# The residual buffers of a two-layer graph kernel: b3 and x brought in by two transfers, the second accumulating, instead of one addition on GpSimd

## The reference

```python
def _sage_conv(x, src, dst, W_l, b_l, W_r):
    agg = segment_sum(x[src], dst, num_segments=N_NODES)
    deg = segment_sum(ones, dst, num_segments=N_NODES)
    return (agg / maximum(deg, 1.0)[:, None]) @ W_l + b_l + x @ W_r

h = relu(_sage_conv(x, src, dst, W1_l, b1, W1_r))
h = relu(_sage_conv(h, src, dst, W2_l, b2, W2_r))
out = _layernorm(x + (h @ W3 + b3))
```

## Time and profile before

| | |
|---|---|
| Three runs, median (lowest to highest) | 3070.76 us (3068.34 to 3070.82) |
| The profiled execution: its time, its span | 3069.83 us, 3068.0 us |
| Granted clock of TensorE over the span | 0.974 |
| Busy: PE, DVE, ACT, POOL | 2858.7, 2459.7, 2066.8, 2239.5 us |
| GpSimd's additions for xb (L390) | 196 of 2402 ns, 470.7 us |
| Bytes moved by DMA | 488.23 MB, mean 159 GB/s |

### The profile page before, as it was taken

The page is one execution under the profiler, slowest core; times in us unless marked ns, Lnnn a source line. Parts: engine busy times, 40 slices in busy tenths (PEclk is TensorE's granted clock), DMA queues, the critical chain, the costliest instruction groups (busy, mean ns, idle before and its releaser), DMA issues. The chain is left out here.

```text
span 3068.0 us, 56367 instructions
## 1 busy us (share of the span) xinstructions
PE 2858.7 (93%) x18433; PEld 2560.7 (83%) x18433; DVE 2459.7 (80%) x4095; ACT 2066.8 (67%) x3188; POOL 2239.5 (73%) x1830
## 2 busy tenths in 40 slices
PE   5999999999999999999999999999998887887885
PEld 4898888888888888888888888888888776777775
DVE  5888888888887878878888788787887876777775
ACT  3777677676766777767767676677776655555554
POOL 5777777777777777777777777777776677777776
PEclk9999999999999999999999999999999898989898
DMA  3444444444444445444444444444443655555553
GB/s 128 147 164 152 156 153 155 150 158 157 157 156 147 161 145 164 151 157 151 155 152 159 156 157 155 146 163 145 164 151 128 211 192 174 193 181 188 194 175 118
DMA packets 253118, 488.23 MB, mean 159 GB/s; under 512 B 37615, under 2 KB 165206, under 8 KB 253090
## 3 DMA queue, kind: packets, MB, share of 16 engines
q1 hardware_dynamic: 202498, 387.58, 37.4%
q0 software_dynamic: 50176, 99.91, 10.8%
q10 hardware_dynamic: 416, 0.40, 0.0%
HBM read 284.67 MB, written 206.22 MB: 160 GB/s over the span
## 5 line engine op out<-in xcount | busy, mean ns | idle before, releaser
L494 ACT ACTIVATE h_full<-pair,bias 128x512 f32<-128x512 f32 x784 | 531.5, 684 | 632.0 <-PE pair L866 616.9
L655 DVE TENSOR_TENSOR h_lo<-h_full,h_hi 128x1024 fp32r<-128x1024 f32 x392 | 658.0, 1679 | 174.7 <-ACT h_hi L496 174.7
L390 POOL TENSOR_TENSOR xb<-xn,b_row 128x1024 f32<-128x1024 f32 x196 | 470.7, 2402 | 225.7 <-DVE y L671 223.8
L344 POOL DMA_INDIRECT xe<-in_x_dram,e_stage x392 | 500.7, 1277 | 177.0 <-issue 97.7
L877 PE MATMUL pair<-w_hi,h_hi 128*128 128x256 f32 x1960 | 553.2, 282 | 30.4 <-DVE h_lo L655 28.7
L877 PE MATMUL pair<-w_hi,h_lo 128*128 128x256 f32 x1960 | 543.0, 277 | 0.0
L877 PE MATMUL pair<-w_lo,h_hi 128*128 128x256 f32 x1960 | 542.5, 277 | 0.0
L856 PE MATMUL pair<-ident,xn 128*128 128x128 f32 x2352 | 336.4, 295 | 128.7 <-DMA xn<-h_tab,c_stage 119.4
L856 PEld LDWEIGHTS pair<-ident,xn 128*128 128x128 f32 x2352 | 301.6, 154 | 163.7 <-issue 115.1
L496 ACT CAST h_hi<-h_full 128x1024 fp32r<-128x1024 f32 x392 | 412.7, 1053 | 12.5
L877 PEld LDWEIGHTS pair<-w_hi,h_hi 128*128 128x128 f32 x1960 | 367.8, 188 | 55.4 <-DVE h_lo L655 51.8
(11 more groups left out here) (117 smaller groups left out, 6583.8 us busy)
## 6 DMA issues: line engine op xcount, KB each, us to landing
xn<-in_x_dram SPq DMA_DIRECT2D x196, 512.0 KB, 3.9
out_dram<-o SPq DMA_DIRECT2D x196, 512.0 KB, 2.7
seg<-seg_tab SPq DMA_DIRECT2D x74, 512.0 KB, 5.0
xdb_tab<-xdb SPq DMA_DIRECT2D x49, 512.0 KB, 4.7
h_tab<-src_h SPq DMA_DIRECT2D x49, 512.0 KB
h_tab<-dst_h SPq DMA_DIRECT2D x49, 512.0 KB, 6.2
xn<-h_tab SPq DMA_DIRECT2D x49, 512.0 KB, 5.2
xb<-xdb_tab SPq DMA_DIRECT2D x49, 512.0 KB, 4.1
```

Source lines behind the costliest of these rows:

```text
L344: nc.gpsimd.indirect_dma_start(out=xe[:, kind, s], out_offset=None, in_=x, in_offset=bass.IndirectOffsetOnAxis(ap=e_stage[:, kind, s:s + 1 ...
L390: nc.gpsimd.tensor_tensor(xb[:, b], xn[:, u], b3_row[:, :].unsqueeze(1).to_broadcast([P, S, D]), ALU.add).then_inc(xb_ok, 1)
L494: nc.scalar.activation(h_full[:, n, k], ps[:, k], ACT.Relu, bias=bias[:, n, k:k + 1]).then_inc(hf_ok[n], 1)
L655: nc.vector.tensor_tensor(h_lo[:, h], h_full[:, n], h_hi[:, h].bitcast(f32), ALU.subtract).then_inc(hlo_ok[n], 1)
```

## The change

The addition on GpSimd is gone. In its place SyncE copies `b3_row` four times over into `xb[u]` (an SBUF to SBUF transfer, counted by `b3_in[u]`), and GpSimd then issues a transfer from DRAM that adds the group's rows of x to what lies there (`accum_op`, counted by `xb_in[u]`), on which the residual waits. xb has four buffers instead of two. Both transfers are for group g + 2: SyncE's waits in body g for the residual of g - 2, GpSimd's for `b3_in`. The load of xn no longer waits for `xb_ok`. Before the loop SyncE issues the b3 copies of all four buffers, ahead of the `slot_tab` transfer, and GpSimd two of the accumulating ones.

```diff
-        xb = sb("xb", [P, 2, S, D])
+        xb = sb("xb", [P, U, S, D])
...
             for u in range(1, U):
                 sp.dma_start(xn[:, u], rows(x, u)).then_inc(x_in[u], 16)
+            sp.wait_ge(b_in, 96)
+            for u in range(U):
+                sp.dma_start(xb[:, u], b3_row[:, :].unsqueeze(1).to_broadcast([P, S, D])).then_inc(b3_in[u], 16)
...
                         sp.wait_ge(xt_ps, (g + 1) * K)
-                        sp.wait_ge(xb_ok, g + 1)
                         sp.dma_start(xn[:, u], rows(x, g + U)).then_inc(x_in[u], 16)
+                    if not (first and u < 2) and not (last and u >= 2):
+                        after(sp, y_ok, g - 1)
+                        sp.dma_start(xb[:, (u + 2) % U], b3_row[:, :].unsqueeze(1).to_broadcast([P, S, D])).then_inc(b3_in[(u + 2) % U], 16)
...
+            def add_x(i, u, ahead):
+
+                i, u = i + (u + ahead) // U, (u + ahead) % U
+                pool.wait_ge(b3_in[u], 16 * (i + 1))
+                nc.gpsimd.dma_start(xb[:, u], rows(x, i * U + u), accum_op=ALU.add).then_inc(xb_in[u], 16)
+
             def body(i, first, last, phase):
                 for u in range(U):
-                    g = i * U + u
-                    b = u % 2
-                    pool.wait_ge(x_in[u], 16 * (i + 1))
-                    after(pool, y_ok, g - 1)
-                    nc.gpsimd.tensor_tensor(xb[:, b], xn[:, u],
-                                            b3_row[:, :].unsqueeze(1).to_broadcast([P, S, D]), ALU.add).then_inc(xb_ok, 1)
+                    if not (last and u >= 2):
+                        add_x(i, u, 2)
...
-            def residual_rows(g, b, ps):
-                dve.wait_ge(xb_ok, g + 1)
+            def residual_rows(i, u, ps):
+                i, u = i + u // U, u % U
+                g = i * U + u
+                dve.wait_ge(xb_in[u], 16 * (i + 1))
                 after(dve, o_ok, g - 1)
-                residual(g, b, l3_ps, y_ok, ps)
+                residual(g, u % 2, u, l3_ps, y_ok, ps)
```

More of the change, by code:

```diff
@@ L127, in build @@
         y_out = [sem(f"y_out{b}") for b in range(2)]
+        b3_in = [sem(f"b3_in{u}") for u in range(U)]
+        xb_in = [sem(f"xb_in{u}") for u in range(U)]
         xt_ps, xhi_ok, xlo_ok = sem("xt_ps"), sem("xhi_ok"), sem("xlo_ok")
@@ L133, in build @@
         hlo_ok = [sem("h1lo_ok"), sem("h2lo_ok")]
-        xb_ok, y_ok, stats_ok, mv_ok, sd_ok, rs_ok, nb_ok, o_ok = (sem(n) for n in (
-            "xb_ok", "y_ok", "stats_ok", "mv_ok", "sd_ok", "rs_ok", "nb_ok", "o_ok"))
+        b3_spread, y_ok, stats_ok, mv_ok, sd_ok, rs_ok, nb_ok, o_ok = (sem(n) for n in (
+            "b3_spread", "y_ok", "stats_ok", "mv_ok", "sd_ok", "rs_ok", "nb_ok", "o_ok"))
         xs_in, xd_in, seg_in = sem("xs_in"), sem("xd_in"), sem("seg_in")
@@ L273, in _ @@
             sp.wait_ge(mean_ok, NI)
-            sp.wait_ge(xb_ok, NG)
             sp.wait_ge(xt_ps, NG * K)
@@ L410, in _ @@
             pool.wait_ge(b_in, 96)
+            add_x(0, 0, 0)
+            add_x(0, 1, 0)
             body(0, True, False, 0)
@@ L414, in _ @@
             body(MIDDLE, False, False, 1)
-            with pool.Fori(MIDDLE + 1, NI - 1) as i:
+            with pool.Fori(MIDDLE + 1, NI - 2) as i:
                 body(i, False, False, 2)
+            body(NI - 2, False, False, 2)
             body(NI - 1, False, True, 2)
@@ L667, in _, with residual @@
             low_x(1, 1, pair[3])
-            def residual(g, b, l3, y_s, ps):
+            def residual(g, b, u, l3, y_s, ps):
                 dve.wait_ge(l3, (g + 1) * K)
                 nc.vector.tensor_tensor(y[:, b].rearrange("p s d -> p (s d)"), ps[:, :, :].rearrange("p k g -> p (k g)"),
-                                        xb[:, b].rearrange("p s d -> p (s d)"), ALU.add).then_inc(y_s, 1)
+                                        xb[:, u].rearrange("p s d -> p (s d)"), ALU.add).then_inc(y_s, 1)
             def moments(g, b, y_s, stats_s, mv_s):
@@ L755, in body @@
                     if not (first and u == 0):
-                        residual_rows(g - 1, (u + 1) % 2, pair[(u + 3) % 4])
+                        residual_rows(i, u - 1, pair[(u + 3) % 4])
                         moments_rows(g - 1, (u + 1) % 2)
@@ L764, in body @@
                     factors_rows(NG - 2, 0)
-                    residual_rows(NG - 1, 1, pair[3])
+                    residual_rows(NI - 1, 3, pair[3])
                     moments_rows(NG - 1, 1)
@@ L803, in residual_edges @@
                 after(dve, c_o_ok, j - 1)
-                residual(j, b, c_l3_ps, c_y_ok, pair[3])
+                residual(j, b, b, c_l3_ps, c_y_ok, pair[3])
                 sums(j, b, c_y_ok, c_stats_ok)
```

## The result

The changed kernel takes 3117.82 us (median of 4 runs, 3116.65 to 3118.71); the kernel before took 3069.55 us beside it (4 runs, 3067.49 to 3070.82). The ratio is 1.0156, with a 95% interval of 1.0141 to 1.0170: 48 us slower, where 28 us faster was forecast, and outside the range of 3022 to 3105.

What follows compares the result with a forecast made beforehand. TensorE was taken to bound the loop, waiting only for VectorE's h_lo, which GpSimd additions delay. Loop gain 36 us, start 5.5 later: -30.5 on 3069.83, 3040, written as 3042; 8 in 10 range 3022 to 3105.

Steps and rivals of the forecast that it cites:

- Floor of the loop: Main loop, TensorE's waits for h_lo: removing them wins 0.95 us of a 47.46 us iteration, 46 us in 48.
- the copy lands after 2.7 to 3.9 us ... I take 2.9, as at that moment nothing else is moving: SyncE's b3 copy in the loop: lands 2.9 us after issue, the load of xn having gone out earlier.
- The other steps up to X: Between y's end and the xdb addition: SyncE's issue 0.25 us behind y, GpSimd's wait 0.4, its issue 1.1.
- X: Start of GpSimd's xdb addition, later counted from y's end (1038.98); forecast at about 1043.6 to 1043.8.
- The price of X: VectorE's second h_lo: delayed by X - 1043.6 for X up to 1045.9, so 0.2 us at X = 1043.8.
- the old formula: VectorE's second h_lo ends at X + 2.42 + 1.08 instead of 1047.13.
- None beyond: VectorE's second h_lo: no delay for X beyond 1045.9, as h_lo is then first and GpSimd waits.
- The bound of 2.3 us on the delay: Second h_lo in the loop: at the worst X the delay is 2.3 us an iteration, a loss.
- rival (1): xdb addition lands on the second h_lo through a later copy or longer issue: 3107 us, chance 0.15.
- Ahead of the loop: Four b3 copies ahead of the slot_tab transfer put the start 5.5 us later, between 3 and 7.
- DMA: Added transfers in the loop: share from 0.47 to 0.73 to 0.86, accumulating taken as double, cost nothing.
- Waits of SyncE and GpSimd in order, edge stage: Work behind SyncE's and GpSimd's new waits, such as stores and gathers, costs nothing; the edge stage is unchanged.

Runs made afterwards that it cites:

- e5: The changed kernel with the xdb addition moved from GpSimd to VectorE (end of its edge work at u = 2), its store to u = 2: 3032.59 us.
- e1: The changed kernel with GpSimd's xdb addition replaced by one over four values and two zero fills that read nothing: 3037.11 us.
- e9: The changed kernel with GpSimd's xdb addition moved ahead of its wait and the accumulating transfer at u = 0: 3040.66 us.
- e3: The changed kernel with GpSimd's transfer of x as a plain copy instead of an accumulating one: 3069.15 us.
- e10: The changed kernel with the b3 copy issued ahead of the load of xn on SyncE, in each body: 3090.09 us.

## Why the prediction was wrong

- **Floor of the loop: right.** 47.46 less 0.95 is 46.51 us; e5 and e1 have 46.61 and 46.57 in the mean, and 46.56 in most iterations. The forecast gain of the removal was there to be had: 48 by 0.9 is 43 us, and e5's trace has 41 of them (2268.2 us from the first y to that of group 195, against 2309.1).
- **The step that failed: "the copy lands after 2.7 to 3.9 us ... I take 2.9, as at that moment nothing else is moving".** With 0.4 for GpSimd's wait, 3.3 us were taken from the issue to GpSimd's going on; measured are 5.31 in the mean for this copy. About 0.65 of that is GpSimd (in e9, where the profile tells these landings, it goes on 0.65 behind), which leaves some 4.7 for the copy. Something else was moving. In the packet records of the iteration shown, the accumulating transfer of the group before has packets from 1010.92 to 1015.83, the load of xn, issued 4.5 us ahead on SyncE, from 1011.79 to 1015.98 beside it, and the copy issued at 1013.91 only from 1015.57 to 1018.11. e3 makes the first of these cheap and wins 0.95 us, e10 takes the second from ahead of the copy and wins 1.02; the two together were not tried. The prediction knew that the load would go out earlier, and took it for over by then. My own estimate of a share of 0.73 to 0.86 should have forbidden a duration read at 0.47.
- **The other steps up to X: three small errors.** SyncE issues the copy 0.03 us behind y, not 0.25. The issue on GpSimd is 0.98 us (1.1 assumed), the longest of the 196 being 1.61, but the addition starts 0.64 behind its start, so that 0.64 counts and not 1.1. GpSimd's wait is 0.65, not 0.4. Together they take 0.4 us off, the copy adds 1.8: X came to 5.98 in the mean against 4.6 to 4.8.
- **The price of X: its zero point was 0.4 us too late.** I let h_lo end at X + 2.42 + 1.08 and no loss begin before X = 4.62. In the trace the addition takes 2.77, not 2.42, and h_lo ends at X + 3.93. Undisturbed it ends 8.19 behind y (e5: 6.96 + 1.23). So the delay is X - 4.26, which gives 1.6 us for X = 5.89; measured 48.31 less 46.56, 1.75. By the old formula it were 1.3. I had overlooked the small `nb` as a victim, and the scan as the thing that TensorE waits for first. `nb` as victim changes the size little, since h_lo ends as far behind the addition where h_lo itself is shut out (X + 3.90 at X = 7.03).
- **"None beyond" X = 1045.9 (6.9 us behind y): wrong.** I took it that h_lo would then be first and GpSimd would wait. At X of 6.92, 7.01 and 7.03 the iterations took 49.21, 49.30 and 49.43 us, the longest of the trace. The bound of 2.3 us on the delay isn't seen up to there; where it ends is not shown.
- **Sum by these terms.** Gain 0.9, loss 1.75 in an iteration: +0.85 by 48, the +40.7 of the table. This is rival (1), which had the place and the sign right, at a chance of 0.15 and 3107 us; most of its case was the length of an issue, while the copy's landing decided.
- **Ahead of the loop: 5.5 assumed, 8.9 measured, one trace against one.** h_full began 7.8 later. The copies were issued behind xn as foreseen, but the slot_tab transfer behind them was later by more than the 1.55 us each that a mean over the span gives, and the first iteration added 1.1. By the spread of the first y given above (68.1 to 75.5 us) the 8.9 could as well be 5 or 12, so this term can't be said to be wrong.
- **DMA: right.** 591 us more of all engines in q0 for 102.8 MB is 5.75 us for a MB, 1.94 times the 2.96 before, close to the double assumed; for the plain transfers of e3, in the same queue, it is 3.13. The b3 copies are 339 us, 1.73 each. The share is 0.86, at my upper end, and by itself harmless (e5, e1, e9 at 0.86 to 0.88, iterations of 46.6 to 46.8). I cost the transfers' load at nothing; it was not nothing for the copy on whose landing the addition waits.
- **Waits of SyncE and GpSimd in order, edge stage: right.** They cost nothing that the traces show; nothing but the xdb addition behind GpSimd's wait counted.

## What to carry to other kernels

When a GpSimd operation that reads SBUF stands behind a wait, the time of that wait places it on VectorE's chain: write down its start as a range, and price each VectorE operation with two SBUF inputs in that range, the smallest too. A median of landings may cover only some of the transfers; read the one that is waited for. A landing time read at one DMA load doesn't hold for a change that doubles the load; ask what will be under way when it is issued. And order the SBUF readers ahead of waits for transfers: here this was worth 77 us, and putting the last one on VectorE 85.

## What the runs showed of the hardware that was not expected

- An operation of 512 values (`nb`, 128x4, 0.16 us) took 2.89 us beside a GpSimd addition: its size is no protection. Nor is its start, when it comes up to 0.36 us ahead of the addition's by the profile.
- An accumulating transfer from DRAM took 5.75 us of all sixteen engines for a MB, a plain one of the same bytes in the same queue 3.13 (e3): 1.84 times. In the packet records of the changed kernel its 4096-byte packets took about 328 ns, plain ones 159.
- GpSimd's issue of such a transfer took 0.98 us (0.57 for a plain one, e3), and its next operation started 0.64 us behind the issue's start. Beside the issue GpSimd's addition took 2.77 us, without it 2.42 (e3) and 2.44 (e9).
- GpSimd's fill of 128x768 values, 1.11 us, left a VectorE operation with two SBUF inputs at its 1.22 us.
- From the issue of a 512 KB copy within SBUF to GpSimd's going on it took from 4.49 to 9.34 us in one and the same kernel, by the body; for the copy of u = 0 it took 5.31, and 4.36 (e3) or 4.29 (e10) with less beside or ahead of it. Four of its issues took SyncE 3.94 us behind three loads.
